# Routed experts: GpSimd squares the units whose low part it forms

## What is computed

```python
x_lat = x @ fc1_w.T                                   # tokens, 128
h = relu2(jnp.einsum('tl,eil->eti', x_lat, w1))       # relu2(x) = square(relu(x))
h = h * cw.T[:, :, None]                              # weight of expert e for token t, mostly 0
y_lat = jnp.einsum('eti,eli->tl', h, w2)
routed = y_lat @ fc2_w.T
shared = relu2(x @ shared_up_w.T) @ shared_down_w.T
```

## Time and profile before

| | us |
|---|---|
| runs, median of 3 | 603.28 (600.13 to 603.64) |
| profiled execution, whole time | 601.21 |
| its span, first to last instruction | 599.4 |
| TensorE matmuls busy | 548.5 (92%) |
| VectorE busy | 401.0 (67%) |
| ScalarE busy | 351.0 (59%) |
| GpSimd busy | 315.4 (53%) |

### The profile page before, as it was taken

The page is one execution under the profiler, slowest core; times in us unless marked ns, Lnnn a source line. Parts: engine busy times, 40 slices in busy tenths (PEclk is TensorE's granted clock), DMA queues, the critical chain, the costliest instruction groups (busy, mean ns, idle before and its releaser), DMA issues.

```text
span 599.4 us, 9600 instructions
## 1 busy us (share of the span) xinstructions
PE 548.5 (92%) x3236; PEld 470.5 (78%) x3242; DVE 401.0 (67%) x828; ACT 351.0 (59%) x716; POOL 315.4 (53%) x301
## 2 busy tenths in 40 slices
PE   1999968998988899999999999999999979889997
PEld 1877746877767799999999999999888758667885
DVE  5868869589856656556565576666774775747675
ACT  2732234566565777756566664667575755767574
POOL 2687345599254677732434434237775635961221
PEclk9999999899988999999999999999999989989999
DMA  8611225310144577797875878535454634336552
GB/s 257 242 54 52 106 87 162 138 37 1 31 164 141 174 247 210 233 280 249 253 249 201 249 241 242 164 124 169 162 191 148 212 122 122 109 97 193 170 170 77
DMA packets 66960, 97.88 MB, mean 163 GB/s; under 512 B 6368, under 2 KB 38880, under 8 KB 66912
## 3 DMA queue, kind: packets, MB, share of 16 engines
q1 hardware_dynamic: 66912, 97.26, 51.4%
HBM read 68.28 MB, written 28.97 MB: 162 GB/s over the span
## 4 chain that ended last, share of the span: by engine, by line
PE 68%; DVE 13%; ACT 5%; POOL 5%; DMA 4%; issue 3%; SPq 1%; DVEq 0%; POOLq 0%; ACTq 0%
PE ps L1486 19%; PE ps L1487 19%; PE ps L1488 19%; PE ps L1582 4%; PE ps L1688 2%; PE ps L1672 1%; DMA cw_row<-cw_scratch 1%; DMA cT_raw<-in_ctx_t 1%; PE ps L1695 1%; DVE a_sel L1132 1%; DMA k_hl<-k_scratch 1%; ACT q2T L880 1%; POOL s_lo L634 1%; DVE h L1071 1%; POOL ex_lo L556 1%
## 5 line engine op out<-in xcount | busy, mean ns | idle before, releaser
L629 POOL TENSOR_TENSOR probs<-probs,rsum 128x512 f32<-128x512 f32 x64 | 66.4, 1041 | 89.4 <-DVE rsum L1198 89.3
L1193 DVE TENSOR_REDUCE nmax<-ps 128x2 f32<-128x512 f32 x64 | 44.1, 688 | 43.6 <-PE ps L1488 43.3
L1413 DVE SCALAR_TENSOR_TENSOR e_r<-ps,cw_row 128x512 f32<-128x512 f32 x64 | 43.9, 687 | 35.7 <-PE ps L1488 32.2
L1003 ACT ACTIVATE e_hi<-e_r 128x512 fp32r<-128x512 f32 x64 | 40.4, 631 | 43.9 <-DVE e_r L1413 43.5
L917 ACT ACTIVATE probs<-ps,nmax 128x256 f32<-128x256 f32 x128 | 59.4, 475 | 7.2 <-DVE nmax L1193 7.1
L556 POOL TENSOR_TENSOR kv_w_lo<-blk_raw,kv_w_hi 128x1024 fp32r<-128x1024 f32 x17 | 41.2, 2422 | 29.0 <-ACT kv_w_hi L793 28.6
L747 POOL TENSOR_TENSOR e_lo<-e_sq,e_hi 128x512 fp32r<-128x512 f32 x22 | 28.4, 1289 | 52.2 <-ACT e_sq L1009 49.8
L1189 DVE TENSOR_TENSOR oT_lo<-ps,oT_hi 128x512 fp32r<-128x512 f32 x32 | 22.1, 692 | 43.9 <-ACT oT_hi L927 43.9
L923 ACT ACTIVATE pT_hi<-ps 128x512 fp32r<-128x512 f32 x64 | 38.2, 598 | 20.5 <-PE ps L1582 20.3
L1184 DVE TENSOR_TENSOR pT_lo<-ps,pT_hi 128x512 fp32r<-128x512 f32 x64 | 43.7, 685 | 5.0 <-ACT pT_hi L923 3.9
L927 ACT ACTIVATE oT_hi<-ps 128x512 fp32r<-128x512 f32 x32 | 19.1, 597 | 44.6 <-PE ps L1488 44.6
(11 more groups left out here) (294 smaller groups left out, 1871.6 us busy)
## 6 DMA issues: line engine op xcount, KB each, us to landing
cw_row<-cw_scratch SPq DMA_DIRECT2D x64, 256.0 KB, 3.3
v_hl<-v_scratch SPq DMA_DIRECT2D x24, 512.0 KB, 3.8
blk_raw<-in_w_blocks SPq DMA_DIRECT2D x23, 512.0 KB, 4.8
k_hl<-k_scratch SPq DMA_DIRECT2D x18, 512.0 KB, 4.0
k_scratch<-kv_out SPq DMA_DIRECT2D x32, 256.0 KB, 2.6
v_scratch<-kv_out SPq DMA_DIRECT2D x32, 256.0 KB, 3.1
v_scratch<-kv_hi SPq DMA_DIRECT2D x24, 256.0 KB, 2.7
blk_raw<-in_w_tail SPq DMA_DIRECT2D x10, 512.0 KB, 4.5
```

What stands on the lines that cost most here:

```text
L629: nc.gpsimd.tensor_tensor(probs[:, b, :, :], probs[:, b, :, :], rsum[:, b, :].unsqueeze(2).to_broadcast([P, 2, S]), ALU.mult).then_inc(pro ...
L1003: nc.scalar.activation(e_hi[i % 4][:, :], e_r[i % 2][:, :], ACT.Square).then_inc(e_hi_done, 1)
L1193: V.tensor_reduce(nmax[:, b, :], ps[:, S_BANK[b], :].rearrange("p (t k) -> p t k", t=2), AX.X, ALU.max, negate=True).then_inc(max_done, 1)
L1413: V.scalar_tensor_tensor(e_r[i % 2][:, :], ps[:, UP_BANK[i % 4], :], 0.0, cw_row[i % 4][:, :], ALU.max, ALU.mult).then_inc(root_done, 1)
```

## The change

For the 22 units of GpSimd, the second square leaves ScalarE. GpSimd makes it itself, as the product e_r x e_r into e_sq, as soon as root(i) is there; it waits for its own result and for ScalarE's e_hi, and then subtracts as before. A new semaphore, squared_by_pool, counts these squares. e_sq_done now counts only the VectorE units, and VectorE's root(i) waits for e_hi and for the second square of unit i - 2, wherever that is made.

```diff
@@ GpSimd, expert_low(i)
                 if i >= NI or not low_on_pool(i):
                     return
-                pool.wait_ge(e_sq_done, i + 1)
+                pool.wait_ge(root_done, i + 1)
+                if lows(i, True) > 1:
+                    pool.wait_ge(low_by_pool, lows(i, True) - 1)
+                nc.gpsimd.tensor_tensor(e_sq[i % 2][:, :], e_r[i % 2][:, :], e_r[i % 2][:, :], ALU.mult).then_inc(squared_by_pool, 1)
+                pool.wait_ge(squared_by_pool, lows(i, True))
+                pool.wait_ge(e_hi_done, i + 1)
                 if i >= 4:
                     pool.wait_ge(down_done, i - 3)
                 nc.gpsimd.tensor_tensor(e_lo[i % 4][:, :], e_sq[i % 2][:, :], e_hi[i % 4][:, :].bitcast(F32), ALU.subtract)\
@@ ScalarE, expert_square(i)
                 nc.scalar.activation(e_hi[i % 4][:, :], e_r[i % 2][:, :], ACT.Square).then_inc(e_hi_done, 1)
                 if not low_on_pool(i):
                     nc.scalar.activation(ps[:, UP_BANK[i % 4], :], e_r[i % 2][:, :], ACT.Square).then_inc(e_sq_done, 1)
-                    return
-                if i >= 2 and low_on_pool(i - 2):
-                    act.wait_ge(low_by_pool, lows(i - 2, True))
-                nc.scalar.activation(e_sq[i % 2][:, :], e_r[i % 2][:, :], ACT.Square).then_inc(e_sq_done, 1)
@@ VectorE, root(i)
                 if i >= 2:
-                    dve.wait_ge(e_sq_done, i - 1)
+                    dve.wait_ge(e_hi_done, i - 1)
+                    if low_on_pool(i - 2):
+                        dve.wait_ge(squared_by_pool, lows(i - 2, True))
+                    else:
+                        dve.wait_ge(e_sq_done, lows(i - 2, False))
                 V.scalar_tensor_tensor(e_r[i % 2][:, :], ps[:, UP_BANK[i % 4], :], 0.0, cw_row[i % 4][:, :],
                                        ALU.max, ALU.mult).then_inc(root_done, 1)
@@ VectorE, expert_low(i)
-                dve.wait_ge(e_sq_done, i + 1)
+                dve.wait_ge(e_sq_done, lows(i, False))
```

More of the change, by code:

```diff
@@ L286, in flamingo_two_layer_kernel @@
             sem("up_filled"), sem("root_done"), sem("e_hi_done"), sem("e_sq_done"), sem("down_done"))
-        low_by_pool, low_by_dve = sem("low_by_pool"), sem("low_by_dve")
+        low_by_pool, low_by_dve, squared_by_pool = sem("low_by_pool"), sem("low_by_dve"), sem("squared_by_pool")
         yl_done, y4_filled, y4_taken = sem("yl_done"), sem("y4_filled"), sem("y4_taken")
```

## The result

The changed kernel takes 608.5 us (median of 20 runs, 602.33 to 609.44) against 601.65 us (598.45 to 607.73, 20 runs): ratio 1.0083, 95% interval 1.0058 to 1.0108, so 5.0 us slower (3.5 to 6.5). The forecast was +4.0 us, or 0.7%, to 607.3 us.

The account below looks back on a forecast made before the run. The prediction took TensorE as the bound (548.5 us, 92% of the span), with GpSimd's queue deciding at two places. Terms 0.5 + 3.4 + 0.1 = +4.0 us on the median 603.28 gave 607.3 us, range 603.0 to 610.5.

Parts of the forecast that it names:

- The dense stretch: Units 31 to 63, TensorE fully busy from 545 to 590 us: squares fit in the slack, 0 us.
- A square costs 1.04 us: Each GpSimd square takes 1.04 us (range up to 1.29) and lengthens its queue by 1.12 us.
- The second place: Units 17 to 25, GpSimd's unbroken run: squares 17, 20 and 22 delay e_lo(22) and TensorE's restart by 3.4 us.
- the last wait for the shared relu: Earlier gap near the second place: VectorE's shared-expert relu comes 1.2 us later behind GpSimd's longer queue.
- The held VectorE queue: Root(24) waits for square 22, holding VectorE's queue by 6.7 us; e_lo(23) and e_lo(24) still come in time.
- The first place: Units 4 and 6, before h's scaling: TensorE restarts 0.8 us later, net +0.5 us (+0.1 to +1.2).
- Behind the second gap: After TensorE's restart, e_lo(25) comes just in time (+0 to +0.3) and the rest shifts along: +0.1 us allowed.
- rival 1: Over 1% slower, deciding from +6.0 us: longer TensorE idle at 524 to 530 us brings more half-clock time, +1.7; chance 0.20.
- The sum: Whole kernel: the terms 0.5, 3.4 and 0.1 give +4.0 us, or 0.7% slower.

Follow-up runs that it names:

- e3: Kernel before, with GpSimd making the second square of only the ten units 34 to 61: 602.46 us, ratio 1.0003.
- e2: Kernel before, with GpSimd making the second square of only units 17, 20 and 22: 606.26 us, ratio 1.0081.
- e4: Changed kernel with four e_r buffers, so that root(i) waits for the square of unit i-4: 607.64 us, ratio 1.0091.
- e1: Kernel before, with GpSimd making the second square of only units 1, 4 and 6: 602.25 us, ratio 1.0016.
- e8: Changed kernel with the split of weight block 29, and the load on SyncE too, moved behind unit 7: 609.1 us, ratio 1.0106.
- e11: Changed kernel with only the split of weight block 29 moved behind unit 7, loads where they were: 605.73 us, ratio 1.0090.
- e9: Kernel before with only the split of weight block 29 moved behind unit 7, loads where they were: 603.8 us, ratio 1.0048.
- e5: Kernel before with the low parts of units 20 and 22 given to VectorE instead of GpSimd: 599.69 us, ratio 0.9957.

## Why the prediction was right

- **The dense stretch gives nothing.** Right. e3, and 45.00 of 45.00 us. The low part of unit 58 ends 3.19 us after its root's start (590.41 to 593.60), before 3.25, so 0.06 earlier; 0.08 was forecast.
- **A square costs 1.04 us and 1.12 us in the queue.** Right, 1.039 and 1.12.
- **The second place, +3.4.** The restart moved by 4.01 - 0.78 = 3.2 us between down(16) and down(22). e2 alone gives 3.1. The step held, a little high. The gap itself grew by 2.2 us, and the last wait for the shared relu by 1.1, as forecast.
- **The held VectorE queue costs nothing.** Right, by e4. It had the longest new wait of all (5.66 us), and it was parallel to the longer one.
- **The first place, net +0.5.** The restart moved by 0.62 (forecast 0.8), e1 gives 0.61. I had taken 0.3 off, since part of the half-clock stretch would fall into the gap. It did not shrink: the stretch was 6.8 us long here, and 4.1 of it lay behind the gap, not less than 3.3. So +0.78 in this execution. In e1, with the same squares, it was 3.4 us long and lay almost wholly in work (3.2), and the stage still grew by 0.61.
- **Behind the second gap, +0.1.** This term was too small. By the clock row TensorE ran 5.2 us there at half clock in place of 3.4; half of 1.8 us is 0.9. The growth from down(22) to down(31) was 0.55: TensorE's last 0.12 us of waiting at down(31) went, and where the remaining 0.2 went the traces don't say. This is the mechanism of rival 1: behind the longer gap a second stretch did follow, at about half of the price of 1.7, since 1.6 us of the 6.8 lay in the gap.
- **What the forecast had against rival 1.** It read from two rows that the half-clock time isn't tied to the gap's length. At the second place the two go together: in all five traces with a gap of 5.5 us (the changed kernel, e2, e4, e8, e11) the stretch is 6.8 us, with 4.4 to 6.1 of it in work; in the four with a gap of 3.4 us it is 3.4 (the kernel before, e1, e9) or missing (e3). Over the runs the granted clock averages 0.978 in the changed kernel (20 runs) and 0.981 in the kernel before (the 92 runs beside the experiments). By the mean spans that is an estimated 4 us more at half clock in an execution; the second place adds 3.4. At the first place they don't.
- **The sum.** 4.0 forecast, 4.5 in stage time, 5.0 (3.5 to 6.5) over the runs. That +4.0 comes so close is in part luck: the errors of the three terms (+0.3, -0.2, +0.45) partly cancel, and over the runs the 5.0 is the mean of two groups, one some 2 us above the kernel before and one some 7, past the +6 from which rival 1 decides. The longer half-clock stretches go the right way for the upper group, whose clock is 0.975 to 0.978 in 11 of 12 runs, where the lower has 0.98 in all 8; but with one trace, of the upper group, the cause of the two groups is not shown.

What stays open: what makes the two groups, and why the first root starts anywhere between 462.2 and 469.0 us in code that is the same. The runs of the kernel before lie up to 9 us apart; how much of that comes from before the first root is not shown, and no experiment was made on it.

## What to carry to other kernels

Moving work to a less busy engine helps only where the bound engine waits for the one relieved; the average busy share (53% for GpSimd) hid a stretch where it had 26.3 us of work in 28.6, and three of the 22 moved operations made most of the loss. The largest entry of the waits view was an idle engine waiting, worth nothing. The cure at the same spot was the reverse, to take work off GpSimd's queue, and when a step is moved later, each queue that waits for its result (SyncE's loads, with other loads behind them) has to be counted too.

## What the runs showed of the hardware

- A product of a tensor with itself on GpSimd, 128x512 float32, takes 1.039 us; a subtraction of two different tensors of that size 1.294. At 128x128 a product of a tensor with itself takes 0.40, of two tensors 0.46.
- VectorE's scaling of h, a tensor_scalar from SBUF to SBUF, 128x256, took 0.40 us alone (0.72 for two in a row) and up to 2.43 with a GpSimd operation in flight; taking that operation away (e9) gave the 2.0 us back. Roots and subtractions that read PSUM kept their 0.69 and 0.68 us beside GpSimd. That is the rule of the Trainium skill's SBUF — State Buffer, Who interferes with whom.
- TensorE's granted clock was 0.50 for 6.8 us around all five idle times of 5.5 us at the second place, with 4.4 to 6.1 us of it in work. Around the four idle times of 3.4 us there it was 0.50 for 3.4 us in three traces, and stayed at 1.00 in e3. At the first place the same 4.2 us of idle had 3.4 us of it in the kernel before and in e2, and 6.8 in e3 and e5. So what a gap costs beyond its length differs between executions.
